# Three more unread matmuls at place 25 and at place 31 of a selective-scan group

## What is computed

```python
def _ssm_layer(x, A_log, Dp, W_dbc, W_dt, b_dt):
    A = -jnp.exp(A_log)                                  # 64 channels x 64 states
    delta, Bm, Cm = split(einsum(x, W_dbc))
    delta = softplus(einsum(delta, W_dt) + b_dt)
    dA = jnp.exp(delta[..., None] * A)
    dBx = (delta * x)[..., None] * Bm[:, :, None, :]
    hs = scan(h_t = dA_t * h_(t-1) + dBx_t)              # over the steps
    y = jnp.einsum('blen,bln->ble', hs, Cm)
    return y + Dp * x
```

## Time and profile before

| | before |
|---|---|
| median of three runs | 6552.89 us |
| profiled execution | 6549.23 us |
| its span, first to last instruction | 6547.1 us |
| mean granted TensorE clock | 0.898 |
| VectorE busy | 6051.5 us (92%) |
| GpSimd busy | 5860.3 us (90%) |
| TensorE matmuls busy | 5116.2 us (78%) |
| ScalarE busy | 4956.5 us (76%) |

### The profile page before, as it was taken

The page is one execution under the profiler, slowest core; times in us unless marked ns, Lnnn a source line. Parts: engine busy times, 40 slices in busy tenths (PEclk is TensorE's granted clock), DMA queues, the critical chain, the costliest instruction groups (busy, mean ns, idle before and its releaser), DMA issues. The chain is left out here.

```text
span 6547.1 us, 115398 instructions
## 1 busy us (share of the span) xinstructions
PE 5116.2 (78%) x35469; PEld 2105.1 (32%) x35469; DVE 6051.5 (92%) x3973; ACT 4956.5 (76%) x10122; POOL 5860.3 (90%) x932
## 2 busy tenths in 40 slices
PE   6878787877878787877878777777777777774787
PEld 2333333333333333333333333333333333331444
DVE  7999999999999999999999999999999999996443
ACT  6888888888888888888888888888888888884222
POOL 7999999999999999999999999999999999994110
PEclk9898989889898989899898998898999999996888
DMA  7888888888887878887787887787888888884000
GB/s 237 259 262 259 263 260 266 261 262 260 260 262 259 263 259 264 260 265 261 259 262 262 259 261 257 260 263 259 264 262 267 261 266 263 262 262 130 5 7 7
DMA packets 560033, 1561.78 MB, mean 239 GB/s; under 512 B 171954, under 2 KB 318002, under 8 KB 559730
## 3 DMA queue, kind: packets, MB, share of 16 engines
q1 hardware_dynamic: 559858, 1559.96, 73.3%
HBM read 1469.03 MB, written 90.59 MB: 238 GB/s over the span
## 5 line engine op out<-in xcount | busy, mean ns | idle before, releaser
L662 POOL TENSOR_TENSOR u<-u,Bt 128x2976 f32<-128x2976 f32 x896 | 5788.7, 6495 | 168.6 <-DMA u<-dx_rows 165.8
L627 DVE TENSOR_TENSOR_SCAN hT<-decay,u 128x744 f32<-128x744 f32 x3584 | 5771.4, 1683 | 136.2 <-ACT decay L468 110.4
L468 ACT ACTIVATE decay<-decay,a_neg 128x371 f32<-128x371 f32 (+2 forms) x7168 | 3636.0, 554 | 616.0 <-PE decay L296 584.0
L296 PE MATMUL decay<-stk,spread 96*128 96x371 bf16 (+2 forms) x7168 | 1914.8, 355 | 1241.8 <-DVE hT L627 1146.7
L314 PE MATMUL z_bank<-hT,Cst 128*32 128x256 f32 x21504 | 1617.3, 423 | 5.2 <-DVE hT L627 3.3
L296 PEld LDWEIGHTS decay<-stk,spread 96*128 96x128 bf16 x7168 | 447.9, 100 | 2805.5 <-DVE hT L627 2600.3
L477 ACT COPY z_sb<-z_bank 128x512 f32<-128x512 f32 x1344 | 805.7, 599 | 385.5 <-PE z_bank L314 385.0
L314 PEld LDWEIGHTS z_bank<-hT,Cst 128*32 128x32 f32 x21504 | 597.3, 116 | 783.7 <-issue 527.3
L1094 POOL TENSOR_TENSOR wr<-pr 128x744 f32<-128x744 f32 x8 | 14.1, 1760 | 395.6 <-DVE pr L1017 395.6
L324 PE MATMUL z_bank<-stk,spread 96*128 96x372 bf16 x1341 | 332.2, 362 | 0.0
L395 PE MATMUL prep_bank<-tmap,yT 64*128 64x32 f32 (+3 forms) x1344 | 252.0, 313 | 13.3 <-DMA yT<-y_rows 13.3
(11 more groups left out here) (164 smaller groups left out, 2599.6 us busy)
## 6 DMA issues: line engine op xcount, KB each, us to landing
u<-dx_rows SPq DMA_DIRECT2D x3584, 372.0 KB, 4.1
delta_parts<-parts SPq DMA_DIRECT2D x112, 279.0 KB, 6.4
stk<-delta_parts SPq DMA_DIRECT2D x112, 279.0 KB, 5.4
y_rows<-z_sb SPq DMA_DIRECT2D x1792, 12.0 KB
yT<-y_rows SPq DMA_DIRECT2D x112, 192.0 KB, 4.4
dx_rows<-dx SPq DMA_DIRECT2D x112, 186.0 KB, 2.6
xT<-in_x SPq DMA_DIRECT2D x64, 186.0 KB, 4.3
xP<-in_x SPq DMA_DIRECT2D x64, 186.0 KB, 4.1
```

What stands on the lines that cost most here:

```text
L296: nc.tensor.matmul(slot[:, e, :, 1:], spread[0:PARTS * QR, TILES_G * q + er // TILES_G, :], src[:, er % TILES_G, :, 1:], start=True, stop= ...
L468: last = nc.scalar.activation(bank, bank, ACT.Exp, scale=a_neg[:, l, c:c + 1])
L627: nc.vector.tensor_tensor_scan(hT[q % 2][:, i * PAIR:(i + 1) * PAIR], pair_slot(p), u[c % RING][:, part * PAIR:(part + 1) * PAIR], 0.0, AL ...
L662: tt(here, here, Bt[buf][:, :].unsqueeze(1).broadcast_to([P, 2 * HALVES * CHUNK, W0]), ALU.mult).then_inc(s_u, 1)
```

## The change

At place 25 `keep_busy` is called once more, with the same arguments as at place 24 and ahead of the four small matmuls of `to_channels`. A new function, `keep_busy_in_prep`, is called at place 31 of each group that has one before it. It waits until the output of `prev` has been copied out of `prep_bank` (`s_post`), and then issues three matmuls of the same shape into that bank. Their results are overwritten by the next projection. Nothing is removed or moved.

```diff
--- before.py
+++ after.py
@@ -324,6 +324,13 @@
                     nc.tensor.matmul(zb[:, 0:W0], spread[0:PARTS * QR, 0, :], stk[buf][0:PARTS * QR, 0, :],
                                      start=True, stop=True)
 
+            def keep_busy_in_prep(at, buf, before):
+
+                pe.wait_ge(s_post, G(before) + 1)
+                for _ in range(3):
+                    nc.tensor.matmul(prep[:, 0:W0], spread[0:PARTS * QR, 0, :], stk[buf][0:PARTS * QR, 0, :],
+                                     start=True, stop=True)
+
             def item(at, buf, i):
                 l, _ = at
                 n = G(at)
@@ -406,7 +413,7 @@
                             fill(here, half, q - 1, i // 2 - 1)
                         elif prev:
                             fill(prev, 1 - half, TILES_G - 1, i // 2 - 1)
-                    if p in (8, 16, 24) or p == 1 and prev:
+                    if p in (8, 16, 24, 25) or p == 1 and prev:
                         keep_busy(here, half, -1 if p == 1 else q - 1)
                     if after and p in (0, 17, 19):
                         item(after, 1 - half, (0, 17, 19).index(p))
@@ -418,6 +425,8 @@
                         times_D(prev, after)
                     if prev and p in (25, 27, 29):
                         to_channels(prev, (25, 27, 29).index(p))
+                    if prev and p == 31:
+                        keep_busy_in_prep(here, half, prev)
 
             first = (0, 0)
             item(first, 0, 0)
```

## The result

The changed kernel takes 6538.7 us (median of 20 runs, 6532.0 to 6546.5) against 6549.0 (20 runs): ratio 0.9985, 95% interval 0.9978 to 0.9991. It is faster by 0.15%, where 1.3% was forecast. Of the signs that the prediction named, the one against it came: two falls of the clock a pair, as before. The profiled execution has a span of 6537.9 us.

What follows compares the result with a forecast made beforehand. VectorE's scan stage was taken to bound the kernel, 149.8 us above its floor through waits after clock falls. Of these 18 + 36 + 11 = 65 stay and 85 go: 6549.2 - 85 = 6464, so 6465 us; range 6425 to 6540.

Steps and rivals of the forecast that it cites:

- What bounds the kernel: Selective-scan stage: VectorE's scans bound it, 5929.0 us for 112 groups, with waits for ScalarE's exponentials after clock falls.
- The floor of 51.60 us a group: Scan stage: 32 undisturbed scans of 1.599 us and 0.43 for a dx product, per group.
- Case D: Whole scan stage: all waits but the start's go, 139 us gained, 6410 us; chance 0.07 with its neighbourhood.
- The edits' own price: Added matmuls at places 25 and 31: 0 at full clock, up to 1.14 us a set at half clock.
- Place 25: Thin stretch behind place 24: nine in ten groups pass without the clock falling; 18 us of loss stay.
- the 149.8 us: Scan stage: its 5929.0 us less 112 groups at 51.60 us, the time that could be won.
- Place 31: Pause at the group's end, cut from 2.71 to about 2.1 us: half the groups still lose 0.64, 36 us stay.
- Rival A: Group's end: the clock still falls there, only the set at place 25 helps; about 6525 us; chance 0.18.
- B: Places 25 to 31: the clock still falls and the new sets run at half clock; 6605 to 6660 us; chance 0.13.
- C: Scan stage: GpSimd and its waits for broadcast rows take over, no change, 6549 us; chance 0.08.

Runs made afterwards that it cites:

- the run with twelve: The changed kernel with twelve unread matmuls at place 31 in place of three, place 25's set kept: 6418.0 us, ratio 0.9801.
- The best run: The changed kernel with twelve unread matmuls at place 31 and five instead of three at each of places 24 and 25: 6411.8 us, ratio 0.9792.
- the memset: The changed kernel with one unread 128 x 256 memset on VectorE behind scan 20 of each group: 6538.3 us.

## Why the prediction was wrong

Point by point, in the prediction's own steps:

- **What bounds the kernel** was right. The floor of 51.60 us a group was met to 0.02 in the run with twelve, and GpSimd did not take over: its waits for rows fell with the stage. Case D, "everything goes", was put at 6410 us; 6412 was reached, but only with two further edits.
- **The edits' own price** of nothing was right. Both sets run in idle time at full clock.
- **Place 25** was right in the count and not in the price. One late fall in ten was to stay; the trace has 11 in 111 intervals, where it had 62. But the prediction split the cost of a pair wrongly. It charged the late fall 1.6 us and the fall at the end 0.31 or 0.97. The clock is at half from 3047 to 3064 without a break, as the slice below shows beside the earlier trace rows. So both waits of the earlier trace rows, 0.99 in front of place 31 and 0.78 in front of place 3 at 3065.90, lie behind the one late fall, which cost 53.90 - 51.60 = 2.30 us. The fall at the end cost 0.31. The sum of a pair is the same, so the error is not in the 149.8 us.

```profile
3060.00:3064.00 4.00, 3.75 (x23) 1.48 (x23) 3.98 (x4) 2.86 (x6) 4.00 (x1) 0.50 0.53 177
```

- **Place 31** is the step that failed: "So I expect falls to go on there, less often [...] I take half the groups at the mean, 0.64: 56 x 0.64 = 36 us." The runs show that three matmuls there do nothing beside place 25 (6537.5 us without them, 6538.7 with them), and that falls at the end became more, 104 for 62, and longer. The stage of the changed kernel is 5920.6 - 5779.2 = 141.4 us above the floor. The best run keeps 15, which leaves about 126 us for the clock. In the pair of the profile both groups lose at the end: 1220.55 - 1114.76 = 105.79, 2.59 over two floors, 1.30 a group. 104 falls at 1.2 us would make 125 of those 126 us. So the number of these falls was taken too low by a factor of two, 56 for 104, and the price as well, 0.64 for about 1.2.
- **The reason behind it** is that the sum took each fall's price for fixed and added up places that are not independent. A kernel without most of its late falls got a fall at the end in nearly every group, and a dearer one, until its pairs had nearly their old length. The prediction had the rows for that doubt: two kinds of group, 53.90 and 51.91 us long, and a fall at the end only where no late fall had come.
- **Rival A** is what happened, "the clock falls at the group's end all the same", and its time of 6518 to 6537 is off by 2 us from the measured 6538.7. That time lies just inside the stated range, whose upper end of 6540 was there for A; it says nothing for the forecast of 6465. A's price of a fall, 0.97, was too low too. B, slower, didn't come: late falls became few, so the new sets rarely came behind one. It does come where twelve matmuls stand at place 31 and none were added at 25, in two of seven executions: 6636 and 6643 us. C fell in the run with twelve: with the clock up the waits for rows went from 159.0 to 51.1 us, and no scan but the first waited for a product.

The page that rival A drew on (the Trainium skill, TensorE: Matmul & The Clock Gate, "A second HAM failure mode: psum-queue depth-cycling") says that idle times between groups of matmuls, though tiny, make the clock swing when they come often enough. The traces agree as far as they go: the clock falls at the end behind a pause of 2.23 us, and late with none over 0.64 between place 24 and the fall. The prediction gave 0.64 as the longest idle time ahead of the late fall; a pause of 1.11 us stands 7 us ahead of it, in front of the spread of place 22 (3039.78). By that page nothing tells which of two equal pauses makes the clock fall, and here that mattered.

**What stays open.** That a length is held is shown. Sixty groups of layer 0 take 3167.9 us in the changed kernel, 3167.5 with place 25 alone, 3168.4 with five matmuls at places 24 and 25, and 3168.5 with the memset. It is not held in all kernels: with place 31 alone they take 3148.0. What holds it is argued, but the traces say more than that the clock has a rhythm of its own. In each of the twelve traces all changes of the granted clock, 55 to 293 of them, lie within 0.01 us of one evenly spaced row of times. The lengths that repeat are whole numbers of its steps: the pair of 105.81 us before, the group of 54.61 with twelve at place 31 alone and the three groups of 157.02 with six to 0.01 us, the pair of 105.79 in the changed kernel to 0.03. The undisturbed group of 51.59 us is not, so such groups shift against this row; with twelve matmuls the late falls of layer 0 come back every nine groups. This fits groups that are lengthened by falls until the loop and the clock's row of times repeat together. It would also explain why the same pause passes in one group and not in another. No run shifted the clock's times against the loop, so it isn't shown. Why three matmuls at place 31 do more without place 25 (6526.9) than with it is not resolved further.

## What to carry to other kernels

When a loop loses time to TensorE's clock, the waits that a profile shows behind one fall are no price list: take one fall away and another can take its time, so fill all thin stretches of the loop before judging one of them. Here the dose counted: with the set of place 25, in the pause of 2.71 us 3 unread matmuls gave nothing, 6 gave 55 us and 12 gave 120. They cost nothing where the engine was idle at full clock; behind a late fall twelve of them cost a wait of 1.05 us. To learn whether a loop has settled at such a length, add a little work to the bounding engine; if the time doesn't move, the engine's own work isn't what sets it. Compare long stretches, not single iterations.

## What the runs showed of the hardware

- Behind a pause of 2.23 us that had 0.63 us of matmuls ahead of it the granted clock fell in 104 of 111 intervals of one kernel, and passed at full in groups of another. With 0.81 us of pause left it fell at the end once in 111. From place 24 to the late fall no pause is longer than 0.64. Of 62 late falls one was left with five added matmuls at place 25, five for three at place 24 and three at place 31.
- A loop of four engines can hold its mean length to 0.6 us in 3168 against 26 us of work added to its bounding engine over all groups, by waits that give way.
- Three more matmuls at place 25 left 11 late falls with three at place 31 and 54 with six there: what a set is worth depends on the falls elsewhere.
- All changes of the granted clock in a trace lie on one evenly spaced row of times, to 0.01 us, and the lengths that repeat (54.61, 105.81 and 157.02 us for one, two and three groups) are whole numbers of its steps, to 0.01 us.
- The same program took two lengths: with twelve at place 31 and none added at 25, executions took 6479 to 6503 us at a mean clock of 0.943 to 0.949, or 6636 and 6643 at 0.899 and 0.898.
